# Three rotating PSUM banks for scores and side work, two-bank row maxima, residual tiles read beside the expert blocks, and gate logits with the gate stationary

## The reference

```
x = x + conv(groupnorm(x))       # a channel gate per image: DCT sums, two small MLPs, sigmoid, scale
t = tokens of x                  # 1024 tokens x 128 channels per image
t = t + attn(layernorm(t))       # 8 heads of 16: softmax(q k^T / 4) v, plus a fixed decay matrix times t'
t = t + ffn(layernorm(t))        # 8 experts, top 2: logits = xf @ wg + bg
  top_vals, top_idx = top_k(logits, 2); gate_w = softmax(top_vals)
  y_e = relu(xf @ w1[e] + b1[e]) @ w2[e] + b2[e];  out = sum over the 2 chosen e of gate * y_e
```

## Time and profile before

| | |
|---|---|
| median of 3 runs | 2376.35 us (2370.98 to 2392.26) |
| the profiled execution, its own time | 2371.68 us |
| its span, from the first to the last instruction | 2369.9 us |
| mean granted TensorE clock | 0.936 |
| busy: TensorE, VectorE, ScalarE, GpSimd | 2076.4, 1897.7, 1460.3, 1019.7 us |
| attention loop, about | 190 to 1870 us |
| expert blocks, about | 1915 to 2288 us |
| final stage | 2289 to 2370 us |

### The profile page before, as it was taken

One profiled execution on the slowest core, in us unless ns is written; L12 is line 12 of the kernel. 1 busy time (PEld: TensorE's weight loads), 2 busy tenths in 40 slices (PEclk: granted clock), 3 DMA queues, 4 the chain that ended last, 5 costly groups with the idle time before them and its releaser, 6 DMA issues.

```text
span 2369.9 us, 35246 instructions
## 1 busy us (share of the span) xinstructions
PE 2076.4 (88%) x11552; PEld 962.0 (41%) x11552; DVE 1897.7 (80%) x3669; ACT 1460.3 (62%) x2897; POOL 1019.7 (43%) x1479
## 2 busy tenths in 40 slices
PE   2699999999999999999999999999999378777743
PEld 1233343433333343334334333333433156666633
DVE  5768799999999999999999999999881366676732
ACT  1127777777777777777787777777674134344410
POOL 2101224444342444434344443433333646777764
PEclk9999999999999999999999999999995688999965
DMA  5330322323132222313222232312012277666659
GB/s 172 55 50 1 55 46 47 91 38 79 29 76 46 47 53 40 76 29 78 46 47 52 41 73 34 77 37 47 15 51 84 77 234 257 205 204 209 209 186 339
DMA packets 100990, 215.06 MB, mean 91 GB/s; under 512 B 30224, under 2 KB 50392, under 8 KB 100376
## 3 DMA queue, kind: packets, MB, share of 16 engines
q1 hardware_dynamic: 78000, 166.96, 28.7%
q0 software_dynamic: 17280, 35.95, 4.3%
q10 hardware_dynamic: 5528, 9.91, 1.2%
HBM read 104.30 MB, written 61.23 MB: 70 GB/s over the span
## 4 chain that ended last, share of the span: by engine, by line
PE 59%; DVE 16%; POOL 8%; DMA 6%; issue 5%; ACT 4%; SPq 1%; ACTq 1%; POOLq 0%; DVEq 0%
PE ps L881 22%; PE ps L893 18%; DVE row_max L1420 11%; POOL y_dram L767 7%; PE ps L860 3%; PE ps L837 2%; ACT region L1170 2%; DMA y_dram<-region 2%; DMA big<-w_dram 2%; DMA region<-y_dram 2%; DVE region L1471 2%; PE ps L845 2%; PE ps L849 2%; PE ps L912 1%; PE ps L925 1%
## 5 line engine op out<-in xcount | busy, mean ns | idle before, releaser
L1420 DVE TENSOR_REDUCE row_max<-ps 128x1 f32<-128x512 f32 x2048 | 1292.3, 680 | 133.4 <-PE ps L860 117.0
L1170 ACT ACTIVATE region<-ps 128x512 f32<-128x512 f32 x2048 | 1093.5, 602 | 377.6 <-PE ps L881 373.0
L860 PE MATMUL ps<-big 48*128 48x512 f32 x2048 | 836.8, 479 | 32.6 <-DMA big<-k_parts 14.7
L881 PE MATMUL ps<-big 50*128 50x512 f32 x2048 | 781.2, 463 | 25.9 <-ACT region L1170 15.0
L881 PEld LDWEIGHTS ps<-big 50*128 50x128 f32 x2048 | 325.9, 191 | 655.9 <-ACT region L1170 505.2
L893 PE MATMUL ps<-region 128*32 128x512 f32 x4096 | 569.7, 629 | 0.0
L860 PEld LDWEIGHTS ps<-big 48*128 48x128 f32 x2048 | 346.3, 193 | 131.8 <-DVE row_max L1420 100.1
L767 POOL DMA_INDIRECT y_dram<-region x284 | 272.0, 958 | 120.0 <-issue 82.6
L713 POOL DMA_INDIRECT xs_dram<-region,slot x256 | 249.2, 974 | 81.2 <-issue 71.8
L649 POOL TENSOR_TENSOR norm_v<-norm 128x8 f32<-128x8 f32 x32 | 6.7, 210 | 573.4 <-DVE norm L1409 573.4
L1021 PE MATMUL ps<-big 128*128 128x512 f32 x284 | 125.9, 443 | 73.2 <-DMA big<-w_dram 72.7
(11 more groups left out here) (183 smaller groups left out, 2032.1 us busy)
## 6 DMA issues: line engine op xcount, KB each, us to landing
big<-w_dram SPq DMA_DIRECT2D x71, 514.0 KB, 4.6
big<-q_parts SPq DMA_DIRECT2D x384, 64.0 KB, 2.4
big<-k_parts SPq DMA_DIRECT2D x372, 64.0 KB, 2.4
region<-xs_dram SPq DMA_DIRECT2D x71, 264.0 KB, 2.9
region<-y_dram SPq DMA_DIRECT2D x16, 1024.0 KB, 10.0
region<-in_x SPq DMA_DIRECT2D x28, 512.0 KB, 5.2
t_dram<-region SPq DMA_DIRECT2D x16, 512.0 KB, 3.4
out<-region ACTq DMA_DIRECT2D x16, 512.0 KB, 6.0
```

Source lines behind the costliest of these rows:

```text
L860: pe.matmul(ps[:, M_BANK + half % M_BANKS, :], lane_rows(q_stack[k % 2], h, SHIFT_ROW)[:, t * P:(t + 1) * P], lane_rows(k_stack[k % 2], h, ...
L881: pe.matmul(ps[:, E_BANK + score % E_BANKS, :], lane_rows(k_stack[k % 2], h, STACK)[:, t * P:(t + 1) * P], lane_rows(q_stack[k % 2], h, ST ...
L1170: act.activation(probs[:, u % 2, step_head(k, s, i), :], ps[:, E_BANK + score % E_BANKS, :], ACT.Exp, scale=DH ** -0.5).then_inc(exp_done, 1)
L1420: dve.tensor_reduce(row_max[:, c, h * TILES + t:h * TILES + t + 1], ps[:, M_BANK + half % M_BANKS, :], AX.X, ALU.max).then_inc(max_done, 1)
```

## The change

It has five parts.

1. **Banks.** Scores and side work share three banks, 0, 1 and 7, and take them in turn in the order in which TensorE issues them. Each waits for the entry three before it: a score's exponential (`exp_done`), or a side operation's emptying (`side_free`). Side operations keep their wait for the side operation before, too. Full scores get four banks, as two pairs.
2. **Maxima.** VectorE reduces both halves in one instruction over two banks; the join and its semaphore go. A full score waits for the maxima of the row of tiles two before.
3. **Logits.** Eight matmuls with a 128x128 tile of t2 stationary and the gate's 8 columns moving become four with the 8 gate columns stationary, each in its own quarter of the array's columns, and 256 tokens moving. ScalarE copies the 128x256 result to `logit_rows`, two transposes bring it back, and VectorE reads those.
4. **Steps.** q moves from 23 and 25 to 27 and 33, k from 33 and 35 to 35 and 37, the second group's maxima from 27 to 25, the logits from 29 to 23; the new transposes stand at 29.
5. **End.** All 16 residual tiles are read beside blocks 8 to 23; results are written over them, and the last five into the first five tiles' places after those are stored.

```diff
-AT_MAX1, AT_MAX1_FIRST = 27, 23
+AT_MAX1, AT_MAX1_FIRST = 25, 23
-AT_PREP = ((1, 3), (15, 17), (23, 25), (33, 35))
+AT_PREP = ((1, 3), (15, 17), (27, 33), (35, 37))
-AT_LOGITS = 29
+AT_LOGITS, AT_TURN_L = 23, 29
+RING = (0, 1, 7)
+def ring_order():
...
+    def take(entry):
+        ring.append(entry)
+        return RING[(len(ring) - 1) % len(RING)], ring[-1 - len(RING)] if len(ring) > len(RING) else ("side", None)
...
+        steps += [(s, "", it, i) for s in range(STEPS) for i in range(HALVES)]
+        for s, kind, j, part in sorted(steps):
+            if kind == "":
+                if 0 <= it * STEPS + s + 1 < IMAGES * STEPS:
+                    early = early or len(order)
+                    at, (of, last) = take(("score", len(score_after)))
+                    score_after.append((at, of, early - 1 if last is None else last))
+            elif 0 <= j < IMAGES:
+                key = (kind, j, part)
+                bank[key], side_after[key] = take(("side", len(order))) if score_after else (RING[-1], ("side", None))
+                order[key] = len(order)
...
+            def take_side(*key):
+                pe.wait_ge(side_free, side_at[key])
+                kind, last = side_after.get(key, ("side", None))
+                if kind == "score":
+                    pe.wait_ge(exp_done, last + 1)
...
             def full_scores(unit, c):
-                half = HALVES * unit + c
-                if half >= M_BANKS:
-                    pe.wait_ge(max_done, half - M_BANKS + 1)
+                if unit >= 2:
+                    pe.wait_ge(max_done, unit - 1)
...
             def scores(k, s, i):
-                score = 2 * (k * STEPS + s) + i
-                if score >= E_BANKS:
-                    pe.wait_ge(exp_done, score - E_BANKS + 1)
+                bank, kind, last = score_after[2 * (k * STEPS + s) + i]
+                if kind == "score":
+                    pe.wait_ge(exp_done, last + 1)
+                else:
+                    pe.wait_ge(side_free, last + 1)
...
             def gate_logits(k):
-                for t in range(TILES):
-                    mm = pe.matmul(ps[:, SIDE_BANK, t * EXPERTS:(t + 1) * EXPERTS], t2[:, t * P:(t + 1) * P], gate_c[:, :],
-                                   start=True, stop=True)
+                for r in range(TILES // 2):
+                    mm = pe.matmul(side("logits", k, 0)[32 * r:32 * r + EXPERTS, 0:2 * P], gate_c[:, :],
+                                   t2[:, 2 * r * P:2 * (r + 1) * P], start=True, stop=True)
+                mm.then_inc(side_ready, 1)
+
+            def turn_logits(k):
+                take_side("turn_l", k, 0)
+                for j in range(2):
+                    mm = pe.transpose(side_tiles("turn_l", k, 0)[:, j, :], logit_rows[:, j * P:(j + 1) * P], ident[:, :])
...
             def maximum(k, n):
-                for c in range(HALVES):
-                    half = HALVES * (k * STEPS + n) + c
-                    dve.wait_ge(full_ready, half + 1)
-                    dve.tensor_reduce(row_max[:, c, h * TILES + t:h * TILES + t + 1], ps[:, M_BANK + half % M_BANKS, :],
-                                      AX.X, ALU.max).then_inc(max_done, 1)
+                dve.wait_ge(full_ready, k * STEPS + n + 1)
+                at = M_BANK + 2 * (n % 2)
+                dve.tensor_reduce(row_max[:, h * TILES + t:h * TILES + t + 1], ps[:, at:at + 2, :], AX.XY,
+                                  ALU.max).then_inc(max_done, 1)
...
-                if T2_FROM <= b < T2_FROM + T2_BUFS:
+                if T2_FROM <= b < T2_FROM + IMAGES:
...
-                if C_BUFS <= k < C_BUFS + IMAGES - T2_BUFS:
-                    sp.wait_ge(result_done, k - C_BUFS + 1)
-                    sp.dma_start(t2_in[k - C_BUFS], t2_dram[k - C_BUFS + T2_BUFS]).then_inc(t2_late, 16)
```

More of the change, by code:

```diff
@@ L125, in max_unit @@
     return g * GROUP + lane * LANE_HEADS + of_lane, t
-def side_order():
-    order = {}
+RING = (0, 1, 7)
+def ring_order():
+    order, bank, side_after, score_after, ring, early = {}, {}, {}, [], [], 0
+    def take(entry):
+        ring.append(entry)
+        return RING[(len(ring) - 1) % len(RING)], ring[-1 - len(RING)] if len(ring) > len(RING) else ("side", None)
     first = [("turn_x", 0, 0), ("turn_x", 0, 1), ("back_n", 0, 0), ("back_n", 0, 1),
@@ L151, in side_order @@
         steps += [(s, "vz", it + 1, b) for b, s in enumerate(AT_VZ if it >= 0 else AT_VZ_FIRST)]
[L152 to L155, removed]
+        steps += [(s, "", it, i) for s in range(STEPS) for i in range(HALVES)]
[9 more added lines that the diff above has]
+                order[key] = len(order)
+    return order, bank, side_after, score_after
 def max_units(it, s):
@@ L848, in values_and_z @@
                     c = b - HALVES
-                    pe.matmul(side, wvz[:, P:2 * P], norm_ch[k % 2][:, c * BANK:(c + 1) * BANK], start=True,
+                    pe.matmul(side("vz", k, b), wvz[:, P:2 * P], norm_ch[k % 2][:, c * BANK:(c + 1) * BANK], start=True,
                               stop=True).then_inc(side_ready, 1)
@@ L906, in back_o @@
                 for t in range(4):
-                    mm = pe.transpose(side_tiles[:, t, :], on_tok[:, 4 * c + t, :], ident[:, :])
+                    mm = pe.transpose(side_tiles("back_o", k, c)[:, t, :], on_tok[:, 4 * c + t, :], ident[:, :])
                 mm.then_inc(side_ready, 1)
             def project_out(k, c):
-                pe.wait_ge(side_free, side_at["out", k, c])
-                pe.matmul(side, wo1[:, :], on_ch[:, c * BANK:(c + 1) * BANK], start=True,
+                take_side("out", k, c)
@@ L913, in project_out @@
+                pe.matmul(side("out", k, c), wo1[:, :], on_ch[:, c * BANK:(c + 1) * BANK], start=True,
                           stop=True).then_inc(side_ready, 1)
             def turn_t2(k, c):
-                pe.wait_ge(side_free, side_at["turn_t2", k, c])
+                take_side("turn_t2", k, c)
                 for t in range(4):
                     at = c * BANK + t * P
-                    mm = pe.transpose(side_tiles[:, t, :], t2[:, at:at + P], ident[:, :])
+                    mm = pe.transpose(side_tiles("turn_t2", k, c)[:, t, :], t2[:, at:at + P], ident[:, :])
@@ L1267, in _ @@
                 act.wait_ge(result_done, k + 1)
-                act.dma_start(out[k], result[k % C_BUFS]).then_inc(stored[k % C_BUFS], 16)
-            for n in range(C_BUFS):
-                act.wait_ge(stored[n], ((IMAGES - 1 - n) // C_BUFS + 1) * 16)
+                act.dma_start(out[k], result[k]).then_inc(stored[k] if k < IN_BIG else stored_late, 16)
+            for n in range(IN_BIG):
+                act.wait_ge(stored[n], 16)
+            act.wait_ge(stored_late, (IMAGES - IN_BIG) * 16)
         @block.vector
@@ L1482, in add_attention @@
                 dve.wait_ge(side_ready, side_at["out", k, c] + 1)
-                dve.scalar_tensor_tensor(t2[:, at], side, b_out[:, 0:1], x_buf[k % X_BUFS][:, at], ALU.add,
+                dve.scalar_tensor_tensor(t2[:, at], side("out", k, c), b_out[:, 0:1], x_buf[k % X_BUFS][:, at], ALU.add,
                                          ALU.add).then_inc(side_free, 1)
```

152 lines of the change are left out of this document (79 added, 73 removed).

## The result

The changed kernel takes 2440.09 us (median of four runs, 2420.07 to 2447.33) where the kernel before took 2373.66 on the same chip (2365.34 to 2392.26). The ratio is 1.0272, with an interval of 1.0226 to 1.0317: slower. The forecast of 2382 was wrong, and so was its range, which ended at 2424. The profiled execution of the changed kernel has a span of 2443.8 us at a granted clock of 0.916 in the mean, against 2369.9 at 0.936 before.

A forecast was written before the change was run, and what follows sets the result against it. The loop's bound was taken to change from unit to unit between TensorE and VectorE. +0.65 us an image, +10 over 15 images, with +3 and -2.9 made +10 on 2371.7: 2382, narrow range 2355 to 2405, wide 2300 to 2424.

The forecast's parts named there:

- Moved steps: In SyncE's queue behind q and k, made 2 to 8 steps later: the later copies delay nothing the loop waits for, cost nothing.
- Logits: At the logits: 1.1 us of work and 1.25 of clock gained an image, +1.3 of bank waits against it, sum -1.05.
- The ring: Score banks shared with side work: scores wait for exponentials two back, +2.4 us an image, +1.1 behind short side work.
- first rival: In the loop, waits for banks fall on time VectorE would take anyway: 2325, four-transpose units 3.0 or less, chance 0.32.
- Maxima: VectorE's two-bank reduction saves 0.09 us a step, 1.2 an image; with 0.6 from moving q and k, -1.8 an image.
- The end: Last stage 6.1 us shorter by four tiles fewer; their reads beside blocks 20 to 23 cost up to 3.2; sum -2.9.
- Image 15: Last image, without full scores: TensorE waits for ScalarE, ten side operations cost about 0.3 each, +3 us (0 to 6).
- second rival: In the loop, ScalarE's delays reach TensorE at once: 2418, units of 3.8 and more at 17, 33, 49, chance 0.2.
- The third: In the loop, short idle gaps between matmul groups lower the clock in every image, 3.4 us each: 2433, chance 0.06.

The follow-up runs named there:

- moved steps alone: The kernel before with only the steps of maxima, q and k moved, its banks, maxima, logits and end as before: 2439.86 us, 1.0324.
- x first: The changed kernel with t2's store and the read of a later image's x ahead of the stack copies in SyncE's queue: 2353.0 us, 0.9938 to the kernel before.
- old logits: The changed kernel with x read ahead of the stack copies, and the eight 8-column logit matmuls of before at step 29: 2392.34 us, 1.0084.
- banks of before: The changed kernel with x read ahead of the copies, single-bank maxima, and three banks for scores, three for full scores, one for side work: 2355.98 us, 0.9937.
- single-bank reductions: The changed kernel with x read ahead of the copies, four full-score banks used singly, two reductions of 512 and the join: 2349.35 us, 0.9915.
- affine at 54: The changed kernel with ScalarE's affine at step 54 in place of 48, SyncE's queue untouched: 2351.31 us, 0.9923 to the kernel before.
- both repairs: The changed kernel with the read of x ahead of the stack copies and the affine at step 54 together: 2354.67 us, 0.9927.

## Why the prediction was wrong

**The step that failed is "Moved steps".** It named SyncE's 48 small copies and what stands behind them, and wrote: "The next thing in SyncE's queue that the loop waits for, the next image's first shift, is made at step 57, twenty steps after the last k: nothing." There is something nearer: the read of a later image's x, in the same queue right behind the copies, due at step 48 and needing 5.1 us to land. It had 6.3 to 7.6 us before, so there were one to two and a half to give; k's copies now come right behind q's and end later, and the read comes 3.9 us later against unit 47 by the moved steps alone, 5.1 in the whole change. Units 49, 51 and 53 of the changed kernel are 6.5 us longer than with x first; twelve images read an x in the loop, which makes 78 of the 87 us between the two medians. The profile of before had all of it: the issue and the start of the affine that waits for it stand 6.35 us apart, and its page has 5.2 for the landing. About half of the 6.5 is the wait itself (3.1), the rest comes behind it, where TensorE runs at 1.2 GHz.

**Without the late read the sum would still have missed, on the other side.** The forecast had +0.65 us an image; with x first it is -0.92 (103.12 less 104.04), and 2353.0 lies just below the narrow range of 2355 to 2405, though inside the wide one. By steps, each against the kernel that lacks only that step:

- Moved steps, apart from x: the moved steps alone lengthen the units outside 49 to 53 by 0.9 an image (unit 27 by 1.38; others change by less, in both directions). The forecast had nothing here, and in its term for the maxima a gain of 0.6 from the move.
- Logits: with the moved steps and the old banks they gave 1.4 (104.04 + 0.9 - 103.51), in the ring 1.8 (104.93 - 103.12). The forecast had 2.35 without ring waits and 1.05 with 1.3 of them: the gain itself came out smaller, and the ring took nothing from it. In time they gave 39, and 15 times 1.8 is 27; the profile with the old logits also took 125.7 us for image 15, where the one with x first took 104.8, a length that varies, as is told below.
- The ring: -0.21 (103.30 - 103.51), where the terms for it added up to +4.8, the 1.3 in the logits included. Its mechanism was right where it was priced: units 1, 3, 5 and 17 to 21 rose by 0.25 to 0.29, for which 0.32 was taken, and all units that rose make +3.5, where the terms before any return make 5.9. What was mis-sized most is what comes back: 3.7, mostly in units that VectorE had held (7, 27, 33, 39, 59), where 1.1 was counted. With the banks of before, weight loads wait for reductions in each of these, 0.3 to 0.7 us in the mean; in the ring, with four full-score banks, in none of them. Whether the fourth bank does that, or the longer units ahead of them, in which VectorE can catch up, was not separated: no run has the ring with three banks for full scores. In the sum this is the first rival with its waits covered almost in full. Its sign did not come, though: units with four transposes are 3.17 and not 3.0 or less, so the waits cost time where they lie, and it comes back in other units. It was measured with the new step positions; with the old ones it was not tried.
- Maxima: the saving was 0.05 a step and not 0.09, and worth 0.18 an image in place of 1.8. Units 39 to 43 did fall, but the new banks did that: they are as short with single-bank reductions, but for 0.13 at step 43.
- The end: the last stage is 5.2 shorter, where 6.1 was taken; the +3.2 in the blocks didn't show.
- Image 15: the +3 can't be judged, since the length of this image varies from trace to trace, as is told below.
- Not priced: the first score of image 0 starts at 142.1 us before (the scores run from there to 1842.7, not from about 190 to 1870) and at 141.6 with the banks of before, but at 135.2 to 137.4 in every kernel with four full-score banks. Image 0's full scores go ahead alone, and get 4 to 6 us from the fourth bank.

**The second rival** (2418) fell: units 17 and 33 are 3.2 and 3.4, not 3.8, and with the affine at 54 unit 49 is 3.19. **The third** gave 2433 and came nearest to the time, for another reason: the clock was down in the loop, but the ring didn't do it, since it stands at 1.00 in the same ring with x read in time. The Trainium skill ("TensorE: Matmul & The Clock Gate", section "A second HAM failure mode: psum-queue depth-cycling") tells of a swing under such small gaps. The four windows with x first, at 1.00 with the ring's gaps in place, do not show it here. The Trainium skill ("PSUM — Partial Sum Buffer", section "Engine vs sequencer instructions") calls ScalarE's queue strictly first in, first out; the exponentials that start only behind the waiting affine, at 1013.96 behind 1012.82, agree.

Every kernel tried in which x comes in time and the logits are the new ones beats both given ones by its interval, the one before by under 1%: six, at 0.9915 to 0.9947. Their intervals overlap, and which is the best stays open.

## What to carry to other kernels

When a step moves, list every DMA that its outcome lets go, and walk on in that queue past them: each later entry has a landing time and a first user, and the slack is the user's start minus the issue minus the landing. A read that waits for nothing of the moved work belongs ahead of it in the queue. And a price for scarcer buffers is only half a price: sum over the units which are lengthened and those in which the engine had waited for something else.

## What the runs showed of the hardware

In the changed kernel TensorE stood for 2.3 to 3.8 us at each of the twelve late reads, and 1.2 GHz followed every time; with the moved steps alone it stood for 1.4 to 2.6 us, and 1.2 GHz followed eight times of twelve. The 256 waits of weight loads for reductions on the banks of before, none over 1.5 us, were not followed by it: the clock of that loop is 1.00 in all four windows. The waits for x so cost about twice their length in the changed kernel (6.5 for 3.1) and less with the moved steps alone (3.2 for 1.9).

Image 15 has full scores beside it only for its first 37 us or so (the last reduction starts at 1745.4 with x first), and TensorE's clock falls in it in every trace, but for how long differs between two kernels with the same work in it. Windows from 1750 to 1830, x first and then both repairs:

```profile
1750.00:1830.00 80.00, 65.24 (x321) 23.20 (x313) 13.28 (x45) 45.68 (x85) 39.31 (x56) 0.84 0.22 81
```

```profile
1750.00:1830.00 80.00, 75.86 (x265) 27.64 (x268) 10.29 (x36) 41.41 (x76) 35.25 (x46) 0.51 0.19 71
```

From its first score to its last, image 15 takes 104.8 us (1708.4 to 1813.2) in the one and 123.5 (1709.4 to 1832.9) in the other, while the fifteen images before it take 1571 and 1572 in all. This is of the size of the spread of each kernel's runs (30 us with x first), and why the spans of single profiles can't be compared here without their stages. What decides it was not found.
